# Attention scores on four groups of 32 rows, with a fourth query/key block and a new order of the attention pass

## The chip, the cores and the metric

The kernel runs on one core of one Trainium2 chip. The metric is the device time of one execution in microseconds.

## What is computed

32 images of 96x96 pixels become 36 patch tokens and a class token each (layer norm, linear, layer norm, positions); with 128 text tokens that is a sequence of 165 rows of 192 values. On it come an attention without softmax (the "linear" one), then the block that this change is about, then an MLP and a top-2 mixture of four experts:

```
h = concat(tokens(x), txt)                       # 32 x 165 x 192
h = h + linear_attention(layernorm(h))           # q k^T / sqrt(192) times v, no softmax
u = layernorm(h)
z = layernorm(u) * g + b
q, k, v = split(z @ in_w.T + in_b)               # 12 heads of 16
attn = softmax(q k^T / sqrt(16))                 # per image and head, 165 x 165
x1 = u + concat_heads(attn @ v) @ out_w.T + out_b
x2 = x1 + mlp(x1);  out = h + x2 + experts(layernorm(x2))
```

## The kernel before

**Stages.** Phase one makes the tokens and both attentions, phase two (from about 690 us) the MLP, routing and experts; the change touches phase one only. Phase one works on pairs of images: 165 rows of each, laid out as three tiles of 128 rows (one of text rows for each image, one with the 37 image-token rows of both at rows 0 and 64). There are 16 pairs. The code of each engine is written out by hand: a set-up with the patches, then `body(0)`, a hardware loop over pairs 1 to 14 and `last_body(15)`; on ScalarE pair 14 stands outside the loop. The engines meet in semaphores that count. There is no planner; the order of the lines in the four `body` functions is the order of work.

**What a pass does.** Body(i) does the softmax attention of pair i and, between its steps, the linear attention and layer norms of pair i+1 (`tokens_T`, `lin_y`, `lin_v`, `lin_m`, `lin_tokens`, `z_T`) and the statistics of pair i+2 (`tokens`). Scores of pair i are made in six units u: three tiles (`TILE_OF`) times two. Each has six heads. TensorE's `scores` (L1937) fills two banks of PSUM with 3 x 165 columns each; VectorE's `maxima` (L1394, one reduction of 990 elements) takes the row minima of the negated scores (`nb`); ScalarE's `exps` (L934) writes the exponentials to `PX` in six instructions; `transpose_probs` (L1970) transposes them on TensorE, 18 groups g of three 128x128 tiles, and the copies `PT` of the groups are shared by ScalarE (odd g) and VectorE (even g). Units with even u use banks 0 and 1, with odd u banks 2 and 3, so that one unit can be filled while the other is read. `contexts_T` (values times probabilities), `contexts` (back to rows), `normed_T` and `project` end a pair; `x1_out` adds the residual.

**Heads and rows.** The product of one head has a contraction of 16. Before, a matmul of `scores` takes a half of 64 rows with four heads, of which three are masked: `queries` (L1017) writes six versions of Q, each with one head of each half left (`own`), with six ScalarE instructions from two blocks of the product `queries_keys`; `keys` (L1404) writes K in five VectorE instructions from two blocks, one of them shared with queries. There are three blocks m of 128 columns: queries 0 to 7, keys 0 to 7, and the last four heads of both. Two 64-row halves of the array work at once.

```
rows = slice(64 * half, 64 * half + 64)
bank, col = 2 * (u % 2) + half, c * S
q, k = Q[rows, 2 * c + u % 2, :], K[rows, c // 2, :, (1 - half) * NIMG:(1 - half) * NIMG + S]
```

**GpSimd** makes the powers for the layer norms (`rstd`: 3 is that before the linear attention, 4 the two behind it, in one instruction) and the addition of the output bias to U (`residual`, UB, L760), on which `x1_out` depends. `w1_high` and `w1_low` split the MLP's and experts' first weights in two parts; two of them stand at the end of pair 14, the others in the last body. `keep_running` issues transposes that nobody reads.

## Time and profile before

| | |
|---|---|
| median of 3 runs (lowest, highest) | 1270.21 us (1269.87, 1274.73) |
| the profiled execution | 1270.14 us |
| its span in the profile | 1268.4 us |
| mean granted clock of TensorE | 0.987 |
| instructions | 27728 |
| busy: TensorE / VectorE / ScalarE / GpSimd | 1176.9 / 875.1 / 745.5 / 410.0 us |
| set-up and first pass / passes 1 to 14 / last pass / phase two | to about 103 / 39.6 us each / 33 us / from 690 us |

The span is that of the profile, and the time is 1.7 us longer, for what lies around it. Busy TensorE time is the union of its matmuls, which are pipelined and whose ends are modelled; it says when TensorE had work, not that it was at its peak. fp32 matmuls are issued as two instructions each. In the rows, L1879 is the helper through which all matmuls go and L1882 that of all transposes, so the names behind the line tell the operation: K,Q are scores, PX the transposes of probabilities, XAT,AT is `lin_y`, PT,VX is `contexts_T`, ZH,wqkr a block of queries and keys, ow,CNT is `project`.

### The profile page before, as it was taken

What the parts mean: (1) busy time and instruction counts of PE and PEld (TensorE: products, weight loads), DVE (VectorE), ACT (ScalarE), POOL (GpSimd) and SP (SyncE); (2) the same over time, 40 slices, a digit from 0 to 9 for tenths busy, and PEclk for the clock granted to TensorE, in tenths of its full rate; (3) what the DMA queues carried; (4) which work ended last, traced back from release to release, by engine and by line L of the source; (5) the groups of instructions that cost most, each with busy time, mean ns of one, the idle gap of its engine ahead of it and who ended that gap; (6) DMA issues with size and microseconds to landing.
All of it is one profiled execution on the core that took longest, in us unless ns stands there. A gap on an engine that the chain in (4) does not pass through costs nothing.

```text
span 1268.4 us, 27728 instructions
## 1 busy us (share of the span) xinstructions
PE 1176.9 (93%) x9709; PEld 1005.2 (79%) x9709; DVE 875.1 (69%) x2380; ACT 745.5 (59%) x1717; POOL 410.0 (32%) x402
## 2 busy tenths in 40 slices
PE   8899989999899998999998999999997999999995
PEld 7777777777777777777776899999886899988995
DVE  4756776667766677666776678777775776777774
ACT  4566555665556654566566755546563666666753
POOL 4520110101101011010100058777668444454454
PEclk8999999999999999999999999999998999999998
DMA  5148221012210122111400533437556566666672
GB/s 212 58 114 220 61 60 52 27 41 60 60 52 28 40 60 60 52 29 39 106 17 36 196 66 73 88 69 198 161 155 152 144 169 179 181 161 166 156 192 27
DMA packets 98554, 127.23 MB, mean 100 GB/s; under 512 B 9735, under 2 KB 90504, under 8 KB 94768
## 3 DMA queue, kind: packets, MB, share of 16 engines
q1 hardware_dynamic: 74911, 105.24, 27.4%
q0 software_dynamic: 23568, 21.06, 11.1%
q8 instruction: 39, 0.64, 0.2%
q14 instruction: 36, 0.29, 0.1%
HBM read 72.49 MB, written 53.72 MB: 100 GB/s over the span
## 4 chain that ended last, share of the span: by engine, by line
PE 39%; issue 35%; DVE 13%; POOL 7%; ACT 3%; DMA 1%; another core or an unknown queue 1%; DVEq 0%; POOLq 0%; ACTq 0%; SPq 0%
PE PS L1879 35%; PE PS L1882 4%; DVE K L1409 2%; POOL UB L765 2%; POOL rs L757 2%; DVE U L1311 1%; POOL expert_rows L861 1%; ACT GF L1184 1%; DVE st L1300 1%; DVE CNT L1438 1%; DVE ZS L1375 1%; DVE ZL L1374 1%; DVE X L1444 1%; DVE Z L1381 1%
## 5 line engine op out<-in xcount | busy, mean ns | idle before, releaser
L1879 PE MATMUL PS<-w2r,GH 128*120 (+1 forms) x828 | 247.8, 363 | 1.9 <-DVE GL L1604 0.7
L1879 PE MATMUL PS<-w2r,GL 128*120 (+1 forms) x828 | 208.4, 252 | 0.0
L898 POOL DMA_INDIRECT out<-YO,ids x94 | 155.8, 1657 | 160.9 <-DVE flag L1820 141.2
L757 POOL TENSOR_TENSOR rs<-ve,minus_half 128x3 f32<-128x3 f32 (+1 forms) x32 | 34.9, 1092 | 503.5 <-DVE ve L1365 343.9
L941 ACT ACTIVATE PX<-PS,nb 128x165 f32<-128x165 f32 x576 | 177.3, 419 | 28.5 <-DVE nb L1397 26.8
L1184 ACT ACTIVATE GF<-PS,b1c 128x480 f32<-128x480 f32 (+1 forms) x216 | 137.4, 637 | 93.6 <-PE PS L1879 77.3
L1879 PE MATMUL PS<-XH,w1r 128*128 128x480 f32 (+1 forms) x432 | 171.7, 400 | 14.5 <-ACT GF L1184 10.9
L1402 DVE COPY PT<-PS 128x384 f32<-128x384 f32 x144 | 79.8, 554 | 112.7 <-PE PS L1882 111.7
L1879 PEld LDWEIGHTS PS<-w2r,GH 128*120 128x120 f32 x828 | 150.5, 182 | 4.7 <-DVE GL L1604 3.2
L1879 PEld LDWEIGHTS PS<-w2r,GL 128*120 128x120 f32 x828 | 152.8, 185 | 0.0
L1882 PE MATMUL PS<-ident,PX 128*128 128x128 f32 x864 | 133.7, 282 | 14.9 <-ACT PT L916 12.3
L1397 DVE TENSOR_REDUCE nb<-PS 128x6 f32<-128x990 f32 x96 | 113.6, 1183 | 46.1 <-PE PS L1879 41.9
L1882 PEld LDWEIGHTS PS<-ident,PX 128*128 128x128 f32 x864 | 94.8, 141 | 52.3 <-issue 21.6
L1879 PE MATMUL PS<-XS,w1r 128*128 128x480 f32 (+1 forms) x432 | 127.6, 377 | 0.0
L1879 PEld LDWEIGHTS PS<-XH,w1r 128*128 128x128 f32 x432 | 82.9, 192 | 43.6 <-ACT GF L1184 28.3
L1614 DVE TENSOR_TENSOR GL<-GF,GH 128x480 fp32r<-128x480 f32 (+1 forms) x150 | 93.6, 629 | 32.1 <-ACT GH L916 28.4
L916 ACT ACTIVATE PT<-PS 128x384 f32<-128x384 f32 x144 | 73.8, 513 | 60.1 <-PE PS L1882 60.1
L1879 PE MATMUL PS<-K,Q 64*128 64x165 f32 (+1 forms) x1536 | 105.4, 313 | 1.5
L861 POOL DMA_INDIRECT expert_rows<-R,dest x88 | 95.0, 1080 | 33.2 <-issue 27.5
L1879 PEld LDWEIGHTS PS<-K,Q 64*128 64x128 f32 (+1 forms) x1536 | 80.1, 159 | 22.2 <-issue 12.6
L1026 ACT ACTIVATE Q<-PS,qb,own 128x330 f32<-128x330 f32 x96 | 53.1, 627 | 75.1 <-PE PS L1879 64.8
L1879 PEld LDWEIGHTS PS<-XS,w1r 128*128 128x128 f32 x432 | 81.3, 192 | 11.9
(295 smaller groups left out, 2279.1 us busy)
## 6 DMA issues: line engine op xcount, KB each, us to landing
w1r<-expert_w_parts SPq DMA_DIRECT2D x25, 1536.0 KB
expert_rows<-empty SPq DMA_DIRECT2D x45, 369.4 KB, 5.5
RT<-expert_rows SPq DMA_DIRECT2D x22, 369.4 KB
X<-x_scratch SPq DMA_DIRECT2D x11, 360.0 KB
out<-X POOLq DMA_DIRECT2D x11, 360.0 KB, 5.6
H<-in_txt SPq DMA_DIRECT2D x16, 192.0 KB
out<-H SPq DMA_DIRECT2D x16, 192.0 KB
x_scratch<-X SPq DMA_DIRECT2D x16, 192.0 KB
```

What stands on the lines that cost most here:

```text
L757: nc.gpsimd.tensor_tensor(rs[:, cols, :].rearrange("p a b -> p (a b)"), ve[:, cols, :].rearrange("p a b -> p (a b)"), eps_half[:, 0:n], AL ...
L861: nc.gpsimd.indirect_dma_start(listd[:, :], bass.IndirectOffsetOnAxis(ap=dest[:, n % 2, t, k:k + 1], axis=0), R[n % RBUF][:, t, :], None, ...
L898: nc.gpsimd.indirect_dma_start(out[:, :], bass.IndirectOffsetOnAxis(ap=ids[:, i, t:t + 1], axis=0), YO[:, i % 2, t, :], None, bounds_check ...
L916: return nc.scalar.activation(dst, src, ACT.Copy, scale=scale)
L941: last = nc.scalar.activation(PX[:, u % 2, c, to:to + S], PS[:, 2 * (u % 2) + r, c * S:(c + 1) * S], ACT.Exp, bias=nb[:, u, 3 * r + c:3 * ...
L1026: last = nc.scalar.activation(to, PS[:, qk_bank(m), 0:2 * SE].rearrange("p (b q) -> p b q", b=2)[:, :, 0:S], ACT.Identity, bias=qb[:, v:v ...
L1184: nc.scalar.activation(GF[:, m % 3, 0:n], PS[:, 2 + m % 2, 0:n], ACT.Gelu, bias=bias, scale=1.0).then_inc(gelu_ready, 1)
L1397: nc.vector.tensor_reduce(nb[:, u, :].rearrange("p (a s) -> p a s", a=2), src, AX_X, ALU.min).then_inc(max_ready, 1)
L1402: cp(*probT_views(g)).then_inc(probT_dve_ready, 1)
L1614: tt(GL[at][:, m, 0:n], GF[:, m % 3, 0:n], GH[at][:, m, 0:n].bitcast(F32), ALU.subtract).then_inc(hid_ready, 1)
L1879: return nc.tensor.matmul(o, l, r, start=start, stop=stop)
L1882: return nc.tensor.transpose(o, x, ident[0:rows, 0:rows])
```

## The change

1. Scores take four groups of 32 rows at once, each with two heads of which one is masked. A step s now makes a whole tile, twelve heads in all four banks, and there are three steps; `score_ps` counts twice in a step, and `maxima` and `exps` still work on half a step. A step s > 0 waits for both exponential blocks of the one before.
2. There are four blocks of queries and keys (bank 3 for the new one), made in the order 0, 1, 3, 2. Q has three versions, written by three ScalarE instructions, and K needs four VectorE instructions. Weights of the blocks grow from 3 to 4 x 128 columns, in the set-up too, where one zeroing of K goes. `project` writes banks 4 and 5 instead of 3 and 4, patch tile 7 bank 1.
3. GpSimd: the power of two norms (`rstd` 4) is split in two instructions, the one that Z needs (5) first; UB waits for XA of the next pair.
4. New order in the bodies of TensorE, ScalarE and VectorE. Among others `lin_in` and `x1_out` stand ahead of the maxima on VectorE, `tokens(i + 2)` ahead of `normedT` and the keys. The weight splits of pair 14 move into the last body, and so do more transposes by `keep_running` (35 to 52 in the last body).

TensorE, start of a pass in the loop, before: scores of one unit, values, scores of the second unit, then transposes of probabilities and of XA, and the third unit.

```order
L1879 MATMUL PS<-K,Q 128x165 [waits k_ready]
L1879 MATMUL PS<-K,Q 128x165 x5
L1879 MATMUL PS<-wvr,ZH 128x192 [waits q_ready]
...
L1879 MATMUL PS<-K,Q 128x165 [waits x1_ready,q_ready]
L1879 MATMUL PS<-K,Q 128x165 x5
...
L1882 MATMUL PS<-ident,PX 128x128 [waits prob_ready]
L1882 MATMUL PS<-ident,PX 128x128 x5
...
L1882 MATMUL PS<-ident,XA 128x128 [waits v_ready]
...
L1879 MATMUL PS<-K,Q 64x165 x12
```

Now (one row here is a matmul, which the trace shows as two instructions; the rest of the values is left out):

```order
L1865 MATMUL PS<-K,Q 128x165 [waits q_ready]
L1865 MATMUL PS<-K,Q 128x165 x3
L1865 MATMUL PS<-K,Q 128x165 [waits q_ready,k_ready]
L1865 MATMUL PS<-K,Q 128x165 x3
...
L1865 MATMUL PS<-K,Q 128x165 [waits q_ready]
L1865 MATMUL PS<-K,Q 128x165 x3
L1865 MATMUL PS<-wvr,ZH 128x192 [waits k_ready,q_ready]
...
L1868 MATMUL PS<-ident,PX 128x128 [waits prob_ready]
L1868 MATMUL PS<-ident,PX 128x128 x5
...
L1868 MATMUL PS<-ident,XA 128x128 [waits v_ready]
...
L1865 MATMUL PS<-K,Q 64x165 [waits prob_ready]
L1865 MATMUL PS<-K,Q 64x165 x23
```

The second unit is gone from between the values and the transposes; the next step of scores stands behind the third transpose and waits for the exponentials (`prob_ready`).

VectorE, end of a pass and start of the next, before: copies of the context (CNT), keys (K), statistics of the text (BN_STATS to ve), then the first reduction, X and XA.

```order
L1438 COPY CNT<-PS 128x384
L1409 TENSOR_SCALAR K<-PS,consts 32x2x37 [waits qk_ps]
L1409 TENSOR_SCALAR K<-PS,consts 32x2x165 x2
L1409 TENSOR_SCALAR K<-PS,consts 64x2x37 [waits qk_ps]
L1409 TENSOR_SCALAR K<-PS,consts 128x2x165
L1300 BN_STATS st<-H 128x6 [waits txt_in]
...
L1305 TENSOR_SCALAR ve<-mv 128x3 [waits dve_step]
...
L1397 TENSOR_REDUCE nb<-PS 128x6 [waits score_ps]
...
L1444 TENSOR_TENSOR X<-PS,UB 128x384 [waits x1_stored]
...
L1311 TENSOR_SCALAR XA<-H,mv,rs 128x192 [waits rstd_ready3]
```

Now, from the last context's product (CN) on:

```order
L1419 TENSOR_TENSOR CN<-PS,rec 128x192 [waits dve_step]
L1295 BN_STATS st<-H 128x6 [waits txt_in]
...
L1300 TENSOR_SCALAR ve<-mv 128x3 [waits dve_step]
L1424 COPY CNT<-PS 128x384 [waits cnT_ps]
...
L1404 TENSOR_SCALAR K<-PS,consts 128x2x37 [waits qk_ps]
L1404 TENSOR_SCALAR K<-PS,consts 128x2x165
L1404 TENSOR_SCALAR K<-PS,consts 128x2x37 [waits qk_ps]
L1404 TENSOR_SCALAR K<-PS,consts 128x2x165
...
L1306 TENSOR_SCALAR XA<-H,mv,rs 128x192 [waits rstd_ready3]
...
L1431 TENSOR_TENSOR X<-PS,UB 128x384 [waits x1_stored]
...
L1392 TENSOR_REDUCE nb<-PS 128x6 [waits score_ps]
```

The statistics moved ahead of CNT and the keys, one key instruction is gone, and XA and X stand ahead of the reductions.

The diff, cut to its core:

```diff
-QK_COLS = list(range(0, 128)) + list(range(D, D + 128)) + [w * D + 128 + 32 * half + e for half in range(2) for w in range(2)
-                                                           for e in range(32)]
+LAST_HEADS = (8, 9, 9, 8, 10, 11, 11, 10)
+QK_COLS = [w * D + e for heads in (range(8), LAST_HEADS) for w in range(2) for h in heads for e in range(h * HD, (h + 1) * HD)]
+QK_ORDER = (0, 1, 3, 2)
...
         def rstd(j, k):
             pool.wait_ge(var_ready[k], j + 1)
-            cols = slice(k - 1, k if k == 3 else k + 1)
...
+            nc.gpsimd.tensor_tensor(rs[:, k - 1, :], ve[:, k - 1, :], eps_half[:, 0:3], ALU.pow).then_inc(rstd_ready[k], 1)
...
+            if lin:
+                pool.wait_ge(xa_ready, i + 2)
             residual(i, first)
             if lin:
+                rstd(i + 1, 5)
                 rstd(i + 1, 4)
...
         def queries(j):
...
+            for v, m in enumerate((0, 0, 2)):
+                act.wait_ge(qk_ps, j * 4 + QK_ORDER.index(m) + 1)
...
         def body(i):   # ScalarE
             exps(i, 0)
+            exps(i, 1)
             probsT(i, 1)
             xaT(i + 1)
-            exps(i, 1)
+            probsT(i, 3)
             lin_y(i + 1, 0)
             lin_y(i + 1, 1)
-            probsT(i, 3)
             exps(i, 2)
             probsT(i, 5)
+            lin_v(i + 1)
+            probsT(i, 7)
             exps(i, 3)
-            probsT(i, 7)
-            lin_v(i + 1)
             lin_m(i + 1)
+            probsT(i, 9)
             exps(i, 4)
-            probsT(i, 9)
             probsT(i, 11)
...
         def scores(i, s):   # TensorE
+            t = TILE_OF[s]
+            if s > 0:
+                pe.wait_ge(prob_ready, i * 6 + 2 * s)
             for c in range(3):
+                if s == 0:
+                    pe.wait_ge(k_ready, i * 2 + 2)
+                    pe.wait_ge(q_ready, i * 3 + max(c + 1, 2))
+                for g in range(4):
+                    rows = slice(32 * g, 32 * g + 32)
+                    q, k = Q[rows, c, :], K[rows, c // 2, :, (1 - g % 2) * NIMG:(1 - g % 2) * NIMG + S]
                     if t < 2:
+                        last = mm(PS[:, g, c * S:c * S + S], q[:, D * t:D * t + P], k[:, t, :])
                     else:
                         for b in range(2):
+                            last = mm(PS[64 * b:64 * b + 64, g, c * S:c * S + S], q[:, D * b + P:D * b + D], k[:, b, :])
+                    if c == 2 and g % 2 == 1:
+                        last.then_inc(score_ps, 1)
...
         def last_body(i):   # ScalarE
             exps(i, 0)
             exps(i, 1)
+            w1_high(1)
             probsT(i, 1)
...
             exps(i, 3)
+            w1_high(2)
             probsT(i, 7)
-            exps(i, 4)
             probsT(i, 9)
             probsT(i, 11)
+            exps(i, 4)
             exps(i, 5)
```

## Rows read from the trace of the kernel before

**Rows 1.** Page, busy time by engine.

```profile
PE 1176.9 (93%) x9709; PEld 1005.2 (79%) x9709; DVE 875.1 (69%) x2380; ACT 745.5 (59%) x1717; POOL 410.0 (32%) x402
```

**Rows 2.** Windows: us, busy (x instructions) by engine, granted clock, DMA.

```profile
301.20:340.78 39.58, 36.38 (x376) 29.08 (x376) 26.89 (x67) 23.06 (x67) 3.91 (x5) 1.00 0.18 48
```

**Rows 3.** Waits in one pass: us, times, longest.

```profile
DVE PT L1402 <- PE PS L1882: 7.0, 4, 2.7
ACT Q L1026 <- PE PS L1879: 4.4, 1, 4.4
...
ACT MT L916 <- PE PS L1879: 1.9, 1, 1.9
```

**Rows 4.** Timeline, start of a pass: start, us, engine, line [idle before <-releaser].

```profile
299.67 1.48 DVE L1409 TENSOR_SCALAR K<-PS,consts 32x330 f32<-32x330 f32 x3
...
301.20 1.11 PE L1879 MATMUL PS<-K,Q 64*128 64x165 f32 x12
...
302.56 0.47 PE L1879 MATMUL PS<-wvr,ZH 128*128 128x192 f32 x2 [0.25 <-ACT Q L1026]
...
302.83 1.19 DVE L1397 TENSOR_REDUCE nb<-PS 128x6 f32<-128x990 f32 x1 [0.35 <-issue]
...
303.93 0.55 DVE L1444 TENSOR_TENSOR X<-PS,UB 128x384 f32<-128x384 f32 x1
...
304.05 1.84 ACT L941 ACTIVATE PX<-PS,nb 128x165 f32<-128x165 f32 x6 [1.54 <-DVE nb L1397]
...
304.66 1.51 DVE L1311 TENSOR_SCALAR XA<-H,mv,rs 128x192 f32<-128x192 f32 x3
...
304.89 1.73 POOL L765 TENSOR_TENSOR UB<-U,consts 128x192 f32<-128x192 f32 x3 [1.48 <-DVE X L1445]
...
305.94 0.88 PE L1882 MATMUL PS<-ident,PX 128*128 128x128 f32 x6
```

**Rows 5.** Timeline, first pass, VectorE.

```profile
66.34 0.96 DVE L1311 TENSOR_SCALAR XA<-H,mv,rs 128x192 f32<-128x192 f32 x3 [0.54 <-POOL rs L757]
```

**Rows 6.** Timeline, middle of the pass.

```profile
308.12 1.07 PE L1879 MATMUL PS<-K,Q 64*64 64x165 f32 x24
...
309.51 2.39 PE L1879 MATMUL PS<-XAT,AT 128*128 128x330 f32 x8
...
316.86 0.73 ACT L916 ACTIVATE VL<-PS 128x384 f32<-128x384 f32 x2
...
326.78 0.55 DVE L1352 TENSOR_TENSOR H<-PS,H 128x384 f32<-128x384 f32 x1
...
329.53 0.56 DVE L1402 COPY PT<-PS 128x384 f32<-128x384 f32 x1
...
329.62 1.89 PE L1879 MATMUL PS<-PT,VX 128*32 128x165 f32 x48
...
330.94 0.96 DVE L1381 TENSOR_SCALAR Z<-H,mv,rs 128x192 f32<-128x192 f32 x3 [0.85 <-POOL rs L757]
```

**Rows 7.** Timeline, end of the pass.

```profile
336.43 0.36 DVE L1432 TENSOR_TENSOR CN<-PS,rec 128x192 f32<-128x192 f32 x1
...
337.03 0.56 PE L1879 MATMUL PS<-ZH,wqkr 128*128 128x332 f32 x2
...
337.89 0.48 PE L1879 MATMUL PS<-ZH,wqkr 128*128 128x332 f32 x2
...
338.37 2.36 DVE L1409 TENSOR_SCALAR K<-PS,consts 32x74 f32<-32x74 f32 x5
...
338.66 2.11 PE L1879 MATMUL PS<-ow,CNT 128*128 128x192 f32 x12
```

**Rows 8.** Chain of waits, last pass: start, us, what.

```profile
658.48 2.26 PE PS L1879 x20
...
681.73 0.77 PE PS L1879 x16
...
690.25 0.57 ACT XH L916
```

More of the change, by code:

```diff
@@ L195, in build_program @@
     qb = sb(one, "qb", [P, 6])
-    Q = sb(one, "Q", [P, 6, 2 * D])
+    Q = sb(one, "Q", [P, 3, 2 * D])
+    sb(one, "spare_one", [P, 3 * 2 * D - 4 * P])
     K = sb(one, "K", [P, 2, 2, NIMG + S])
@@ L801, in _ @@
         patch_tokens(4)
+        rstd(0, 5)
         rstd(0, 4)
@@ L1072, in body @@
             probsT(i, 15)
+            probsT(i, 17)
             contextsT(i, 0)
-            probsT(i, 17)
             contextsT(i, 1)
             zT(i + 1)
-            if not more:
-                w1_high(1)
-                w1_high(2)
             queries(i + 1)
@@ L1142, in _ @@
         body(0)
-        with act.Fori(1, PAIRS - 2) as i:
+        with act.Fori(1, PAIRS - 1) as i:
             body(i)
-        body(PAIRS - 2, more=False)
         last_body(PAIRS - 1)
@@ L1278, in pair_biases @@
             dve.wait_ge(const_in, 16)
-            steps.link(tt(qkb[:, :], qkb[:, :], PS[:, 1, 2 * D:2 * D + 3], ALU.add))
+            steps.link(tt(qkb[:, :], qkb[:, :], PS[:, 1, 2 * D:2 * D + 4], ALU.add))
             tt(vb[:, :], vb[:, :], PS[:, 1, D:2 * D], ALU.add).then_inc(setup_dve, 1)
-            ts(qb[:, 0:4], own[:, :], qkb[:, 0:1], None, ALU.mult)
-            ts(qb[:, 4:6], own[:, 0:2], qkb[:, 2:3], None, ALU.mult)
+            ts(qb[:, 0:2], own[:, 0:2], qkb[:, 0:1], None, ALU.mult)
+            ts(qb[:, 2:3], own[:, 0:1], qkb[:, 2:3], None, ALU.mult)
             nc.vector.memset(mx[:, 0, 0:1], 0.0).then_inc(h1_stored, 1)
@@ L1404, in keys @@
         def keys(j, m):
-            dve.wait_ge(qk_ps, j * 3 + (0, 3, 1)[m])
-            def part(src, to, at, key, n):
-                cols = PS[src, qk_bank(m), 0:2 * SE].rearrange("p (b q) -> p b q", b=2)[:, :, key:key + n]
-                return ts(K[to, m - 1, :, at:at + n], cols, qkb[src, m:m + 1], -HEAD_SCALE, ALU.add, ALU.mult)
-            if m == 1:
-                part(slice(64, P), slice(64, P), 0, P, NIMG)
-                last = part(slice(0, P), slice(0, P), NIMG, 0, S)
-            else:
-                part(slice(96, P), slice(64, 96), 0, P, NIMG)
-                part(slice(32, 64), slice(0, 32), NIMG, 0, S)
-                last = part(slice(96, P), slice(64, 96), NIMG, 0, S)
+            dve.wait_ge(qk_ps, j * 4 + QK_ORDER.index(m) + 1)
+            for at, key, n in ((0, P, NIMG), (NIMG, 0, S)):
+                cols = PS[:, qk_bank(m), 0:2 * SE].rearrange("p (b q) -> p b q", b=2)[:, :, key:key + n]
+                last = ts(K[:, m // 2, :, at:at + n], cols, qkb[:, m:m + 1], -HEAD_SCALE, ALU.add, ALU.mult)
             last.then_inc(k_ready, 1)
@@ L1485, in body @@
             contexts(i, 2)
-            normedT(i)
-            keys(i + 1, 2)
-            keys(i + 1, 1)
-            if not more:
-                w1_low(1)
             if more:
                 tokens(i + 2)
+            normedT(i)
+            keys(i + 1, 1)
+            keys(i + 1, 3)
         def last_body(i):
             maxima(i, 0)
+            maxima(i, 1)
             x1_out(i - 1)
             values(i)
-            maxima(i, 1)
             probsT(i, 0)
+            probsT(i, 2)
             maxima(i, 2)
-            probsT(i, 2)
             maxima(i, 3)
             probsT(i, 4)
+            w1_low(1)
+            probsT(i, 6)
+            probsT(i, 8)
+            maxima(i, 4)
+            maxima(i, 5)
             w1_low(2)
-            probsT(i, 6)
-            maxima(i, 4)
-            probsT(i, 8)
             probsT(i, 10)
-            maxima(i, 5)
             probsT(i, 12)
@@ L1553, in _ @@
         dve.wait_ge(qk_zeroed, 1)
-        keys(0, 2)
         keys(0, 1)
+        keys(0, 3)
         tokens(1)
@@ L1907, in biases @@
             pe.wait_ge(lin_bias_ready, 1)
-            for m in range(3):
+            for m in range(4):
                 for k in range(2):
@@ L2128, in body @@
         def body(i, first=False):
+            if first:
+                pe.wait_ge(yvar_ready, PTILES - 1)
             scores(i, 0)
             values(i)
-            if first:
-                pe.wait_ge(yvar_ready, PTILES - 1)
-            scores(i, 1, first)
+            if not first:
+                pe.wait_ge(x1_ready, i)
             transpose_probs(i, 0)
```

138 lines of the change are left out of this document (52 added, 86 removed).

## The prediction

> **What bounds the kernel now.** I read the page first for the balance, then the stretches, then the waits and the timeline of one pass. TensorE is busy 1176.9 of the 1268.4 us [rows 1], so a reader might stop there. The stretches are more telling: one pass of the attention loop (one pair of images) takes 39.58 us, in which TensorE is busy 36.38, VectorE 26.89, ScalarE 23.06 [rows 2]. No engine is full, and "busy" counts pipelined ends. The waits of that pass show TensorE and its partners waiting in turns: VectorE's copies of probabilities wait 7.0 us for TensorE, ScalarE's queries 4.4 [rows 3]. It is a ring of hand-overs, and a pass lasts as long as its longest ring. I cut the ring at the moment when VectorE's last key instruction ends (301.14) and call it 0; the next one is at 340.73 [rows 4, 7]. All T below count from there. Three marks of the pass before: the first transposes of probabilities at T 4.8 (305.94), the second transposed context product ends at T 30.4 (329.62 + 1.89) and the ring closes at T 39.6, so the parts are 4.8, 25.6 and 9.2 us [rows 4, 6, 7].
>
> **Part 1: the score products.** A unit before has 12 instructions (6 matmuls in two passes) on 64-row halves and takes 1.11 us [rows 4]; with the last one's 0.30 us latency off, that is 0.81/11 = 74 ns each. The middle units, on 64x64 quarters, issue 24 in 1.07 us [rows 6]: 0.77/23 = 33 ns each. So two pieces of the array side by side give 74 ns, four give 33 ns. After the change a step is 24 instructions on four 32-row groups, or 48 on eight pieces (four row groups, two column halves) for the middle tile. I price each of the three steps at 1.1 us, the row of four pieces. Bounds: 24 at 74 ns is 2.0 us; below, eight pieces at 17 ns and four at 33 give again 1.1. TensorE then has three units where it had six, 3 x 1.05 = 3.2 us less work a pass, against one more query/key block, five matmuls from 337.03 to 337.89 or 0.86 us [rows 7].
>
> What this rests on: the trace's loads of 128 columns come 74 ns apart on two row groups, so loads of different row groups run beside each other. The Trainium skill, "TensorE: Matmul & The Clock Gate", section on LDWEIGHTS, says that a load costs its columns over 1.2, whatever its rows: an estimate of 107 ns for 128 columns, and if loads were one at a time a step would be 24 x 107 ns = 2.6 us and the change a loss. The trace does not agree with loads one at a time.
>
> **Part 2: queries and keys.** Queries: six activations become three, and ScalarE waits 4.4 us there anyway [rows 3]: nothing on the path. Keys: five instructions in 2.36 us become four; the one left out has 330 elements, 0.57, leaving 1.8. It is on the path: -0.57.
>
> **Part 3: order on VectorE.** The statistics of the next text stood behind the keys: from 301.14 to the reduction at 302.83 are 1.69 us, of which 0.35 are marked issue (the loop's branch) and 1.34 the statistics [rows 4]. Now they stand in the tail, ahead of the context's last copies: +1.34 there, and gone from behind the keys. Then come the normalisation (XA), the residual (X), and only then two reductions. XA's three instructions take 1.51 us in the loop, but 0.96 in the first pass, where they run before GpSimd's UB additions [rows 4, 5]; in the loop UB's 1.73 us run beside them. The change lets UB wait for XA, so I take 0.96. Left beside it, it would cost 0.55 more a pass.
>
> **Part 4: the walk of the new pass.** VectorE: branch 0.35, XA 0.96, X 0.85 (0.73 to the next start, and its drain), reduction 1.19 makes T 3.4. ScalarE's exponentials of the first half (1.84) end at 5.25, and the transposes start at 5.3: **+0.5** against 4.8. TensorE stands idle from about 3.7 (project until 0.5, scores 1.1, values 2.26 [rows 8]), so the first step's price is covered by VectorE up to some 1.6 us.
> From 5.25: second exponentials 1.84 (7.1); the second score step must wait for them, as it overwrites both halves: 0.2 + 1.1 (8.4); transposes 0.3; the 330-column product 2.4 with 0.15 to its second half's copy, copy 0.45 (11.65); exponentials 1.84 (13.5); copy 0.5, value copies 0.73, copy 0.5, exponentials 1.84 (17.1); third score step 0.2 + 1.1, reduction 1.19, exponentials 1.84 (21.5); transposes 0.55, copy 0.56 (22.6); the H addition with its statistics, 326.78 to 329.53, 2.75 (25.4); copy 0.56, two transposes 0.9 (26.9), context product 1.89 = 28.8 [rows 6]. The part lasts 23.5 us where it was 25.6: **-2.1**. It gains because three score units and their switches of array shape left TensorE's queue, and because the two waits of ScalarE between exponentials shrink (1.9 us for MT alone [rows 3]).
> Tail: from there Z is ready and not waited for (0.85 for GpSimd's power before [rows 6]), so the last CN is done 4.4 later, where it took 5.3 (to 336.43 + 0.36 [rows 7]); statistics 1.34, two CNT copies 1.05, keys 1.8: T 37.45, with 0.1 for starts. **-0.5** against 9.2. TensorE's projection (2.11 us [rows 7], 0.2 to start) then ends at T 0.5, and the scores start behind it, as the walk has it. The split of GpSimd's power of six columns (1.33) into two of three costs nothing: z_out stands behind a copy of probabilities.
> A pass: 37.5, so -2.1.
>
> **Part 5: ends.** First pass: the fourth block delays the scores by 0.8, but the two exponential blocks end as early as they must; its gain is 1.6. The 13 common passes: 13 x 2.1 = 27.3. The last loop pass has no statistics, so their move gives nothing: 1.8. Last body: ScalarE's high parts of two weight blocks and VectorE's subtractions move in between the exponentials, where ScalarE has to be on time. There T 0 before is 657.1 (the values' start 658.48 [rows 8] less the 1.4 that lie between 301.14 and 302.56 in the loop [rows 4]). By the same kind of walk the second context product ends at T 28.2, where it was at 682.5 - 657.1 = 25.4 [rows 8]: +2.7. Everything behind 690.25 [rows 8] is unchanged. Moved copies of high weights gained nothing before: they stood where ScalarE waited.
> Sum: -1.6-27.3-1.8+2.7 = **-28.0 us**. The profiled execution took 1270.14 against a median of 1270.21, so the sum holds for the median: 1242.
>
> **Rivals.**
> *Scores pace themselves* (loads or passes of row groups overlap only in pairs). For: no row has four row groups; 64-row halves give 74 ns. Against: four quarters give 33. Price: 24 x 74 ns + 0.3 = 2.1 us and 48 x 33 ns + 0.3 = 1.9; the first step is half covered, the two others add 1.0 and 0.8: a pass of 39.2, that is 15 x 1.7 = 25.5 given back, **1268**.
> *The gate on both halves* (slower side). Before, one half of the score banks is filled while the other is read. Now every step waits for two exponential blocks, 3.7 us, and TensorE has to live on transposes and the linear attention of the next pair, whose copies sit on ScalarE between those same exponentials. The middle is a chain of some 20 hand-overs; I gave each 0 to 0.1 us. If each costs 0.1 more the 2.1 us are gone, and at 0.15 more a pass is 0.9 longer than before: 15 x 0.9 + 2.7 = 16, **1286**. For: copies of probabilities wait 7.0 us a pass [rows 3]. Against: VectorE and ScalarE are each idle for over 12 us [rows 2].
> The Trainium skill, "TensorEngine Tiling (Array Packing)", section "PSUM Bottleneck", warns that tiling speeds TensorE and not the emptying of PSUM; the rows of the reductions and exponentials agree, since they cost the same as before.
> *A shorter ring* (the moved work fills waits better, and the last body doesn't lose): 36.6 a pass and nothing lost at the end: 15 x 3.0 = 45, **1225**.
>
> **How the numbers follow.** Forecast 0.62 (1242; its own range 1230 to 1258 is +-1 us a pass), shorter ring 0.14, pace of scores 0.10, gate 0.08, something between forecast and no change 0.06. A measurement of this kernel tells about 0.5% (6.4 us) from no change. Faster: 0.62 + 0.14 + 0.05 = 0.81. Same: most of the score rival and what is left between, 0.10. Slower: 0.09. The range for 8 in 10, 1226 to 1262, leaves out half of the shorter ring, the gate and most of the score rival.
>
> **What the new profile should show.** Passes 37.5 us apart; the score steps 24 and 48 instructions in about 1.1 us (over 1.7: rival one); XA in 0.96, UB behind it; TensorE idle some 1.6 us ahead of the first transposes, with the granted clock at 1.00 as in the pass before [rows 2]; a last body longer by 2 to 3 us. I am wrong if a pass is above 38.6, or if the steps are cheap and ScalarE and VectorE wait longer than before in the middle (rival two).

## The result, and the profile after

The changed kernel takes **1227.51 us** (median of 4 runs, 1225.09 to 1228.78); the kernel before, run beside it on the same chip, 1270.97 us (4 runs). The ratio is 0.9651, 95% interval 0.9625 to 0.9677, and the medians differ by 43.5 us, where 28 were forecast. Ratios here and below are of the means of the fast runs; one run of the kernel before, in the second group of the experiments, was a slow one (1421.43 us at a granted clock of 0.75) and is not among them. The span of the profiled execution is 1226.3 us, against 1268.4. Its busy time, as in [rows 1]:

```profile
PE 1142.6 (93%) x9810; PEld 982.8 (80%) x9810; DVE 854.3 (70%) x2364; ACT 718.1 (59%) x1669; POOL 413.5 (34%) x417
```

Where the time came from, stretch by stretch, cut in both traces at the end of VectorE's last key instruction:

| stretch | before | after | forecast |
|---|---|---|---|
| set-up, to T 0 of the first pass | 62.13 | 63.45 | +0.8, in the next row |
| first pass | 41.4 | 38.2 | -1.6 |
| each of the 13 common passes, mean | 39.56 | 36.27 | -2.1 |
| last loop pass | 39.2 | 36.2 | -1.8 |
| last body, to XH | 33.2 | 38.4 | +2.7 |
| behind it | 578.2 | 578.5 | 0 |

The sum is 1.3 - 3.2 - 13 x 3.29 - 3.1 + 5.2 + 0.3 = -42.3 us; the spans differ by 42.1. So each pass gains half as much again as forecast, and the last body loses twice as much. Of the set-up's 1.3 us a part is clock: from 59 to 63 us the granted clock is 0.57 in the changed kernel, with 0.50, the lower of its two levels, in the middle of it; the kernel before has 1.00 from 58 to 62.

The windows of one pass (against [rows 2]), of the last body, and of five microseconds in it:

```profile
355.54:391.81 36.27, 33.92 (x383) 27.44 (x382) 25.46 (x66) 21.31 (x63) 4.24 (x6) 1.00 0.19 52
609.39:647.85 38.46, 31.07 (x363) 25.61 (x362) 24.45 (x45) 21.36 (x58) 1.69 (x3) 0.96 0.02 8
614.40:619.40 5.00, 3.67 (x17) 3.13 (x17) 2.14 (x6) 3.92 (x10) 1.69 (x3) 0.66 0.15 51
```

TensorE is busy 33.92 us where it was 36.38, so 2.5 us of its work are gone from a pass that is 3.3 shorter. The granted clock is 1.00 in the pass, and 0.66 shortly after the last body's start; within those five microseconds it is 0.50 for 3.2 us (615.72 to 618.95). The waits of the same pass (us, times, longest), against [rows 3]:

```profile
DVE PT L1397 <- PE PS L1868: 7.0, 7, 2.4
...
ACT Q L1025 <- PE PS L1865: 4.1, 2, 2.5
ACT PX L944 <- DVE nb L1392: 3.9, 2, 3.6
```

The start of the pass on the timeline (T 0 is 355.54), against [rows 4]:

```profile
354.12 1.42 DVE L1404 TENSOR_SCALAR K<-PS,consts 128x74 f32<-128x74 f32 x4
...
354.46 2.12 PE L1865 MATMUL PS<-ow,CNT 128*128 128x192 f32 x12
...
355.46 0.95 DVE L1306 TENSOR_SCALAR XA<-H,mv,rs 128x192 f32<-128x192 f32 x3
...
356.51 1.12 PE L1865 MATMUL PS<-K,Q 32*128 32x165 f32 x24
...
356.73 0.56 DVE L1431 TENSOR_TENSOR X<-PS,UB 128x384 f32<-128x384 f32 x1 [0.33 <-PE PS L1865]
...
357.21 0.35 DVE L1432 TENSOR_TENSOR X<-PS,UB 128x192 f32<-128x192 f32 x1
...
357.67 2.28 DVE L1392 TENSOR_REDUCE nb<-PS 128x6 f32<-128x990 f32 x2
...
357.70 1.71 POOL L765 TENSOR_TENSOR UB<-U,consts 128x192 f32<-128x192 f32 x3 [3.49 <-DVE X L1432]
...
360.79 0.88 PE L1868 MATMUL PS<-ident,PX 128*128 128x128 f32 x6 [0.98 <-ACT PX L944]
```

The 24 score instructions take 1.12 us. They end at 357.63, and VectorE, whose X ends at 357.56, begins its reduction at 357.67: two engines arrive there within 0.1 us of each other. Both had to wait for the projection, which ends at 356.58. XA takes 0.95, and no gap is marked between the keys and it, though the loop's branch lies there. The other two score steps, the two context products, and the tail with the statistics, against [rows 6, 7]:

```profile
362.57 1.11 PE L1865 MATMUL PS<-K,Q 32*64 32x165 f32 x48
...
372.49 1.12 PE L1865 MATMUL PS<-K,Q 32*128 32x165 f32 x24
...
381.34 0.87 PE L1868 MATMUL PS<-ident,PX 128*128 128x128 f32 x6 [0.58 <-DVE PT L1397]
...
382.14 1.89 PE L1865 MATMUL PS<-PT,VX 128*32 128x165 f32 x48
...
387.88 0.36 DVE L1419 TENSOR_TENSOR CN<-PS,rec 128x192 f32<-128x192 f32 x1
...
388.15 0.87 DVE L1295 BATCH_NORM_STATS2 st<-H 128x6 f32<-128x192 f32 x3
...
389.49 0.55 DVE L1424 COPY CNT<-PS 128x384 f32<-128x384 f32 x1
```

Which of the two engines sets the pace from the tail to the first reduction is told by the chain of waits. In the kernel before it goes through VectorE's keys:

```profile
339.25 0.57 DVE K L1409
```

In the changed kernel it stays on TensorE for 6.8 us without a gap, through the query and key blocks, the projection and the scores, and touches neither the statistics nor the keys:

```profile
387.10 1.83 PE PS L1865 x10
388.93 0.44 PE PS L1868 x4
389.37 4.55 PE PS L1865 x46
...
393.94 1.20 DVE nb L1392
```

The marks of the pass are therefore T 5.25 (first transposes, 360.79), T 28.5 (382.14 + 1.89) and T 36.27; the parts are 5.25, 23.24 and 7.8 us, where 5.3, 23.5 and 8.7 were forecast. The last body, against [rows 8]:

```profile
615.72 1.12 PE L1868 MATMUL PS<-ident 128*128 128x128 f32 x4 [2.01 <-DVE VX L1386]
...
616.63 2.40 PE L1868 MATMUL PS<-ident,PX 128*128 128x128 f32 x9
...
629.94 1.81 DVE L1437 TENSOR_TENSOR w1r<-rw,w1r 128x768 fp32r<-128x768 f32 x2
...
632.37 0.84 PE L1868 MATMUL PS<-ident,PX 128*128 128x128 f32 x6 [1.50 <-DVE PT L1397]
```

Ahead of the first transposes TensorE waits 2.01 us for the values' copy; then nine instructions of transposes take 2.40 us, where six take 0.88 in the pass. Later it waits 1.50 for a copy that stood behind a weight subtraction.

### The profile page after: what moved, and what is told of

The parts are those of the page before. It is cut to its first block, busy times and chain, and to the rows that moved or that the text cites. A ratio compares the mean times of both kernels' runs of the same rounds, so it can differ in the third digit from the quotient of the medians.

```text
span 1226.3 us, 27879 instructions
## 1 busy us (share of the span) xinstructions
PE 1142.6 (93%) x9810; PEld 982.8 (80%) x9810; DVE 854.3 (70%) x2364; ACT 718.1 (59%) x1669; POOL 413.5 (34%) x417
## 4 chain that ended last, share of the span: by engine, by line
PE 66%; DVE 12%; issue 9%; POOL 6%; ACT 5%; another core or an unknown queue 1%; DMA 1%; POOLq 0%; ACTq 0%; SPq 0%; DVEq 0%
PE PS L1865 52%; PE PS L1868 13%; POOL expert_rows L864 4%; ACT PX L944 2%; DVE nb L1392 2%; ACT GF L1179 1%; DVE PT L1397 1%; POOL out L852 1%; DVE st L1354 1%; DVE H L1350 1%; POOL lex L857 1%; DVE ZS L1370 1%; DVE ZL L1369 1%; DVE H L1347 1%
## 5 line engine op out<-in xcount | busy, mean ns | idle before, releaser
L944 ACT ACTIVATE PX<-PS,nb 128x165 f32<-128x165 f32 x576 | 174.1, 417 | 59.3 <-DVE nb L1392 59.3
L758 POOL TENSOR_TENSOR rs<-ve,minus_half 128x3 f32<-128x3 f32 x48 | 40.5, 854 | 423.2 <-DVE ve L1359 318.2
L1868 PE MATMUL PS<-ident,PX 128*128 128x128 f32 x864 | 136.8, 284 | 30.9 <-ACT PX L944 17.0
L1392 DVE TENSOR_REDUCE nb<-PS 128x6 f32<-128x990 f32 x96 | 112.1, 1184 | 39.8 <-PE PS L1865 38.4
L1233 ACT ACTIVATE YO<-PS,cs 120x192 f32<-120x192 f32 x94 | 39.3, 419 | 80.3 <-PE PS L1865 69.1
L919 ACT ACTIVATE GH<-GF 128x480 fp32r<-128x480 f32 (+1 forms) x141 | 83.5, 592 | 4.5
L1865 PE MATMUL PS<-XL,w1r 128*128 128x480 f32 (+1 forms) x216 | 81.1, 376 | 0.0
```

Source lines behind the costliest of these rows:

```text
L758: nc.gpsimd.tensor_tensor(rs[:, k - 1, :], ve[:, k - 1, :], eps_half[:, 0:3], ALU.pow).then_inc(rstd_ready[k], 1)
L919: return nc.scalar.activation(dst, src, ACT.Copy, scale=scale)
L944: last = nc.scalar.activation(PX[:, u % 2, c, to:to + S], PS[:, 2 * (u % 2) + r, c * S:(c + 1) * S], ACT.Exp, bias=nb[:, u, 3 * r + c:3 * ...
L1233: nc.scalar.activation(YO[:, at, t, :], PS[0:TB, 4 + t, 0:D], ACT.Copy, scale=cs[:, i, t:t + 1]).then_inc(high_out, 1)
L1392: nc.vector.tensor_reduce(nb[:, u, :].rearrange("p (a s) -> p a s", a=2), src, AX_X, ALU.min).then_inc(max_ready, 1)
L1865: return nc.tensor.matmul(o, l, r, start=start, stop=stop)
```

## The experiments

They ran in three groups, each beside the kernel before: in the first group it takes 1258.06 us, in the second 1267.69, in the third 1258.66. The first group had one chip, the second and the third another one, the same for both. What compares is the ratio to the kernel before in the same group. "The changed kernel on the same chip" means its ratio (0.9651, again 0.9639) times that time. Pass lengths are from one GpSimd addition UB to the next; "XH at" is where the attention phase ends in the profiled execution (690.25 in the kernel before, 647.8 in the changed one), so that it can be compared without what lies behind. It still holds the set-up, which differs a little from run to run: the first UB of the profiled executions lies at 67.1 to 70.2 us.

| kernel | median us (runs) | ratio [95%] | a pass | XH at |
|---|---|---|---|---|
| changed, again | 1223.0 (4) | 0.9639 [0.9615, 0.9663] | 36.27 | 647.3 |
| dose0 | 1228.07 (4) | 0.9759 [0.9743, 0.9775] | 37.10 | 660.4 |
| dose12 | 1242.07 (4) | 0.9872 [0.9849, 0.9895] | 37.94 | 673.4 |
| tokens_back | 1251.03 (4) | 0.9945 [0.9929, 0.9962] | 37.97 to 40.75 | 681.0 |
| tokens_back_busy | 1247.53 (4) | 0.9845 [0.9822, 0.9869] | 37.99 | 668.2 |
| w1_back | 1216.05 (4) | 0.9665 [0.9649, 0.9681] | 36.27 | 647.7 |
| last_new | 1217.23 (4) | 0.9604 [0.9584, 0.9623] | 36.27 | 641.0 |
| act14 | 1218.46 (4) | 0.9605 [0.958, 0.9629] | 35.96 | 645.7 |
| best | 1205.13 (5) | 0.9572 [0.9554, 0.959] | 35.97 | 637.5 |
| x_first_wait | 1224.94 (4) | 0.9735 [0.9716, 0.9754] | 36.93 | 656.8 |
| x_first_free | 1231.8 (4) | 0.9792 [0.9771, 0.9813] | 37.48, one 38.93 | 664.4 |
| before_tokens | 1262.28 (7) | 1.0034 [1.0023, 1.0045] | 39.82 | 694.4 |

### dose0 and dose12: what a score step costs

The matmuls of the first step (dose0), or of the second and third (dose12), are issued twice, the second time over the same result.

```diff
-            for c in range(3):
+            for rep, c in [(rep, c) for rep in range(2 if s == 0 else 1) for c in range(3)]:
...
-                    pe.wait_ge(q_ready, i * 3 + max(c + 1, 2))
+                    pe.wait_ge(q_ready, i * 3 + (3 if s == 0 else max(c + 1, 2)))
...
-                    if c == 2 and g % 2 == 1:
+                    if rep == (1 if s == 0 else 0) and c == 2 and g % 2 == 1:
                         last.then_inc(score_ps, 1)
```

dose12 has `s > 0` in these places. In dose0 the first step also waits for the third version of Q from its first matmul on. That costs nothing in the trace: the step starts 0.92 us behind the keys' end, in the changed kernel 0.97. In dose12 the changed wait has no effect.

> The changed kernel, with every matmul of the first score step issued twice (same result), in all 16 passes. One step is six rounds of 0.14 us, so TensorE gets 0.84 us more a pass. Theory A (the forecast's: VectorE's XA, X and reduction cover the first step up to some 1.6 us): 0 to +2 us in all. Theory B (read from the new trace, where project ends, the step starts at once and the reduction starts on its end: the tail of the ring runs through TensorE): 16 x 0.84 = +13 us.

> The changed kernel, with every matmul of the second and third score step issued twice, which brings TensorE's score work a pass to 5 steps where it has 3 now. Theory A (score steps of the middle lie on the ring, as the walk has them): 2 x 0.84 x 16 = +27 us. Rival (ScalarE's and VectorE's chain of copies and exponentials paces the middle, TensorE has room): under +10 us.

dose0's first step and the reduction behind it:

```profile
360.61 1.96 PE L1865 MATMUL PS<-K,Q 32*128 32x165 f32 x48
...
362.61 2.29 DVE L1392 TENSOR_REDUCE nb<-PS 128x6 f32<-128x990 f32 x2 [0.95 <-PE PS L1865]
```

The second helping adds 0.84 us to the step, VectorE now waits 0.95 for it, and the pass is 37.10 instead of 36.27, longer by just that 0.84. In all it costs 13.9 us against the changed kernel's 1214.2 on this chip, for 13 expected of theory B. The forecast's cover of 1.6 us is not there: the step is on the ring in full. The two steps of dose12 become 1.95 and 1.96 us and the pass 1.67 longer, so they are on the ring in full too (27.9 us in all, for 27 expected). Together the three steps move the pass by what they cost. Read backwards, and as an estimate: had four pieces side by side been no faster than two (steps of 2.1, 2.1 and 1.9 us, the forecast's first rival), a pass would be some 2.8 us longer, and little of the 3.3 us gained would be left. By that estimate the gain hangs on the four row groups running beside each other. No run has the new order with 64-row halves, or the row groups in the old order.

### tokens_back and tokens_back_busy: the statistics in the tail

On VectorE the statistics of pair i+2 go back behind the keys, all else as in the changed kernel. The second kernel adds 14 transposes that nobody reads (into bank 5), ahead of the first transposes of a pass.

```diff
-            if more:
-                tokens(i + 2)
             normedT(i)
             keys(i + 1, 1)
             keys(i + 1, 3)
+            if more:
+                tokens(i + 2)
...
                 pe.wait_ge(x1_ready, i)
+                keep_running(5, 14)     # tokens_back_busy alone
             transpose_probs(i, 0)
```

> The changed kernel, with the text's statistics (tokens) on VectorE moved back behind the keys. Theory: the tail is 1.3 us shorter, but XA, which now stands first in the next pass, has to wait for the statistics (1.3) and GpSimd's power (0.85), so X and both reductions come some 2 us later: +0.8 us a pass, +11 in all. Rival (the place of the statistics doesn't matter, since TensorE's project ends the tail anyway): within 3 us of the changed kernel.

> The kernel tokens_back (1251 us where the changed one is some 1214 on the same chip) with 14 idle transposes (1.5 us) ahead of the first transposes of a pass, where TensorE stood idle 2.8 us. In tokens_back 38.0 us was a pass at granted clock 1.00, and about a third of the passes took 39.3 to 40.8 at 0.92 to 0.96. Theory A (the long idle time costs clock): all passes 38.0 at 1.00, 10 to 15 us faster than tokens_back. Rival (the long passes come from transfers or from elsewhere): no change, or slower by what the transposes cost.

tokens_back, end of a pass, start of the next, and two passes in windows:

```profile
407.90 0.56 DVE L1424 COPY CNT<-PS 128x384 f32<-128x384 f32 x1 [1.16 <-PE PS L1868]
...
412.57 0.96 DVE L1306 TENSOR_SCALAR XA<-H,mv,rs 128x192 f32<-128x192 f32 x3 [0.97 <-POOL rs L758]
...
417.28 1.54 PE L1868 MATMUL PS<-ident,PX 128*128 128x128 f32 x6 [2.71 <-ACT PX L944]
```

```profile
180.66:220.18 39.52, 35.44 (x383) 28.56 (x381) 25.48 (x66) 21.39 (x63) 4.21 (x7) 0.96 0.17 48
373.65:414.40 40.75, 36.69 (x384) 29.79 (x381) 25.48 (x66) 21.51 (x63) 4.22 (x7) 0.92 0.17 46
```

Taken out of the tail, the statistics shorten it by almost nothing: VectorE then waits 1.16 us for the transposed context. From the last CN to the end of the keys are 3.51 us, against 3.57. Behind the keys they cost themselves and 0.97 us of GpSimd's power in addition: the first reduction starts 3.9 us behind the keys instead of 2.1. That is the 1.7 us of the 37.99 us passes, twice what was expected of the order. Then TensorE is idle for 2.7 us ahead of the first transposes in every pass, and five of the 13 passes have a granted clock of 0.92 to 0.96 and last 39.3 to 40.75 us. In these five the clock is at 0.50 for some 3 to 7 us, beginning within about 1 us of the end of that wait; the other eight have 1.00 throughout. tokens_back_busy fills that idle time and does nothing else:

```profile
255.13:293.12 37.99, 35.47 (x398) 28.95 (x396) 25.49 (x66) 21.31 (x63) 4.22 (x6) 1.00 0.18 50
```

All its passes take 37.97 to 38.01 us. The ratio falls from 0.9945 to 0.9845, which is 12.7 us, and XH comes 12.8 us earlier. The two kernels ran on different chips, but the traces agree with the ratios: 8.6 us of it lie in those five passes, 1.5 ahead of the first UB, the rest at the end. So about a third of tokens_back's 37 us was the clock, and the rest mostly the order. The changed kernel's idle stretch at that place is 0.98 us, and its passes keep 1.00.

### before_tokens: the same move in the kernel before

```diff
+            if more:
+                tokens(i + 2)
             normedT(i)
...
             keys(i + 1, 1)
...
-            if more:
-                tokens(i + 2)
```

> The kernel before the change with the statistics of the text moved ahead of normedT and the keys, as in the change, and nothing else. Theory (that order suits the new structure only: in the old one the reduction waits for the scores anyway, so it starts some 0.4 us sooner, while the tail grows by 0.8): +0.4 us a pass, 5 us slower than before. Rival (the move is a gain of its own, the statistics leave the ring): 0.5 to 1 us a pass faster.

```profile
339.84 0.55 DVE L1437 COPY CNT<-PS 128x384 f32<-128x384 f32 x1
...
344.46 1.19 DVE L1397 TENSOR_REDUCE nb<-PS 128x6 f32<-128x990 f32 x1 [1.21 <-PE PS L1879]
```

The ratio is 1.0034 [1.0023, 1.0045], 3 to 6 us more, as expected, and a pass is 39.82 against 39.58. From CN's end to the keys' end are 4.65 us instead of 3.94: CNT no longer waits, but that wait was only 0.53 and the statistics are 1.34. Behind the keys no more than 0.48 is won, since the reduction needs the scores, which need the last key and take 1.11: it starts 1.21 behind the keys instead of 1.69. So the move that is worth 1.7 us a pass in the new structure costs 0.24 in the old one, where the statistics filled a wait for the scores.

### x_first_wait and x_first_free: XA, X and GpSimd's UB

Both put the residual X ahead of XA on VectorE; the second also takes away GpSimd's new wait for XA.

```diff
-            lin_in(i + 1)
             x1_out(i - 1)
+            lin_in(i + 1)
...
-            if lin:                          # x_first_free alone
-                pool.wait_ge(xa_ready, i + 2)
```

> The changed kernel with X ahead of XA on VectorE, GpSimd's UB still waiting for XA. Theory: X can start only when project ends (1.2 us after the keys), so the 0.95 us of XA, done in that gap now, come behind it: reductions 0.8 us later, 37.1 us a pass (if TensorE's longer idle time costs no clock), +12 us in all. Rival (the place of XA is free): 36.3.

> As x_first_wait, but GpSimd's UB no longer waits for XA, so it runs beside XA. Theory (they share a way to the SBUF, as the 0.96 and 1.51 us of XA before the change say): XA 1.5 us, 0.55 us more a pass than x_first_wait, 37.6 us, +8 us. Rival (GpSimd costs XA nothing): the same as x_first_wait.

X, XA and UB of one pass in x_first_wait, then in x_first_free:

```profile
359.45 0.56 DVE L1431 TENSOR_TENSOR X<-PS,UB 128x384 f32<-128x384 f32 x1 [1.17 <-PE PS L1865]
...
360.19 0.95 DVE L1306 TENSOR_SCALAR XA<-H,mv,rs 128x192 f32<-128x192 f32 x3
...
361.36 1.70 POOL L765 TENSOR_TENSOR UB<-U,consts 128x192 f32<-128x192 f32 x3 [4.41 <-DVE XA L1306]
```

```profile
365.37 1.51 DVE L1304 TENSOR_SCALAR XA<-H,mv,rs 128x192 f32<-128x192 f32 x3
...
365.59 1.74 POOL L765 TENSOR_TENSOR UB<-U,consts 128x192 f32<-128x192 f32 x3 [3.47 <-DVE X L1430]
```

X first costs 0.66 us a pass, and 9 us in all by XH, 11 to 12 by the ratios (12 expected): X waits 1.17 us for the projection, and XA, which has nothing to wait for, no longer fills that time. With UB free to run beside XA, its three instructions take 1.51 us instead of 0.95, and the pass is longer by just that, 37.48 against 36.93. So the effect that the forecast read from [rows 4, 5] is real and worth 0.55 us a pass. But in the changed kernel the order alone should secure it: UB waits for X (3.49 us above), X stands behind XA, and the added wait has nothing left to do in the loop. That follows from the code and the trace; the changed kernel without that wait alone was not tried.

### w1_back, last_new: the last body

w1_back puts ScalarE's high parts of weight blocks 1 and 2 and VectorE's subtraction of block 1 back to the end of pair 14; the subtraction of block 2 stays in the last body. last_new does this too and reorders the last body: X ahead of the maxima, no wait for the values' copy ahead of the first transposes, exponentials 2 and 4 a copy earlier on ScalarE, the subtraction of block 2 ahead of the copy and the two reductions that it stood behind, and the idle transposes shared out anew (34 for 32 in these places).

```diff
             queries(i + 1)            # ScalarE, pair 14
+            if not more:
+                w1_high(1)
+                w1_high(2)
...
             keys(i + 1, 3)            # VectorE, pair 14
+            if not more:
+                w1_low(1)
...
+            x1_out(i - 1)             # VectorE, last_new
             maxima(i, 0)
             maxima(i, 1)
-            x1_out(i - 1)
...
             values(i)                 # TensorE, last_new
-            pe.wait_ge(v_ready, i + 1)
-            keep_running(6, 4)
             pe.wait_ge(x1_ready, i)
             transpose_probs(i, 0)
             transpose_probs(i, 1)
+            pe.wait_ge(v_ready, i + 1)
+            keep_running(6, 2)
```

> The changed kernel, with the high parts of weight blocks 1 and 2 (ScalarE) and the low part of block 1 (VectorE) put back at the end of pass 14, as before the change; block 2's low part stays in the last body. The last body took 33.2 us before and 38.5 after. Theory A (ScalarE's 1.6 us copies stand between exponentials and delay them): 3 to 5 us faster than the changed kernel, about 1223. Rival (the order of TensorE's steps and its extra idle transposes cost it): within 1 us of the changed kernel.

> The changed kernel with a last body of another order: weight blocks 1 and 2 high and 1 low at the end of pass 14; X of pair 14 ahead of the reductions; the first transposes no longer wait for the values' copy; each score step as soon as the exponentials allow; block 2 low after the sixth copy. In the changed kernel the last body takes 38.5 us, with a stretch in which the granted clock is 0.66 after TensorE waited 2.0 us for the values' copy. Theory (waits of my list and the lost clock make it long, not the added idle transposes): the second context product ends at T 24 instead of 30.7 and the granted clock stays 1.00: 5 to 7 us faster than the changed kernel. Rival (the chain of exponentials sets it): under 2 us.

w1_back, block 2's subtraction and the wait for the copy behind it, then two windows; then two windows of last_new:

```profile
628.62 1.81 DVE L1439 TENSOR_TENSOR w1r<-rw,w1r 128x768 fp32r<-128x768 f32 x2
...
631.05 2.13 PE L1871 MATMUL PS<-ident,PX 128*128 128x128 f32 x9 [1.97 <-DVE PT L1399]
```

```profile
613.00:618.00 5.00, 3.65 (x17) 3.20 (x17) 2.14 (x6) 2.47 (x8) 1.68 (x3) 0.66 0.15 51
628.00:633.00 5.00, 3.02 (x19) 2.20 (x17) 3.46 (x5) 4.44 (x14) 0.00 (x0) 0.84 0.00 0
```

```profile
608.00:641.50 33.50, 29.78 (x366) 24.37 (x365) 23.75 (x44) 18.80 (x55) 2.07 (x6) 1.00 0.03 9
610.00:615.00 5.00, 3.63 (x47) 3.05 (x54) 3.95 (x7) 3.95 (x13) 1.71 (x3) 1.00 0.15 51
```

w1_back is not faster (0.9665 for the changed kernel's 0.9651, 1.8 us, inside the intervals; XH at 647.7 for 647.8, but from the UB of pair 14's pass to XH it takes 73.8 us for 72.6). The 1.2 us more are clock: behind its second wait nine transposes take 2.13 us and a context product 2.68, where 1.68 and 1.89 are usual, so by this estimate the body would be as long as in the changed kernel. Sending back the high parts and block 1's subtraction gives nothing. The first wait is still 2.01 us, with the clock at 0.66 behind it, and later there is a wait of 1.97 us with 0.84 around it. That second wait is for a copy right behind block 2's subtraction, as the 1.50 in the changed kernel is, and w1_back left this subtraction where it was. So it does not clear VectorE's subtractions as a whole.

In last_new TensorE waits at most 1.3 us there, and the clock is 1.00 throughout. From the UB of pair 14's pass (573.32; 575.23 in the changed kernel) to XH are 67.7 us instead of 72.6: -4.9, and -4.4 by the ratio to the changed kernel in the same group. That is just short of the 5 to 7 expected, and the second context product ends at T 25.8, where T 24 was expected. The last body's loss is thus in the order of its hand-overs, block 2's subtraction among them, with the clock as a part of the price: nine transposes at 2.40 instead of 1.68 us and four at 1.12 instead of 0.60 are 1.2 us. How much each of last_new's moves gives was not taken apart.

### act14: the ring's last hand-over of the middle

Copy 14 of the probabilities goes from VectorE to ScalarE, since the transposes at 381.34 wait 0.58 us for VectorE.

```diff
-ON_ACT = (1, 3, 5, 7, 9, 11, 13, 15, 17)
+ON_ACT = (1, 3, 5, 7, 9, 11, 13, 14, 15, 17)
```

> The changed kernel with copy 14 of the transposed probabilities on ScalarE instead of VectorE, where it stood behind the 2.7 us of lin_out while TensorE waited 0.6 to 0.8 us for it. Theory (that wait is on the ring): about 0.35 us a pass, 5 us in all. Rival (next in line is ScalarE's own copy 15, or the tail): 0 to 1 us.

```profile
379.27 0.93 PE L1868 MATMUL PS<-ident,PX 128*128 128x128 f32 x6 [0.25 <-ACT PT L919]
```

The wait falls to 0.25, a pass to 35.96 (-0.31), the ratio to 0.9605, 4 to 6 us less than the changed kernel (5 expected). The intervals of the two ratios overlap; it is the passes that show the gain. VectorE's copies wait 7.0 us a pass for TensorE, and yet at this one place it is TensorE that waited for a copy.

### best: both, and the first weight block earlier

best is last_new with act14, and the first weight block's split moved between the exponentials of the last body.

> The order of last_new with copy 14 on ScalarE (act14), and in the last body block 0's high part ahead of copy 9 and its low part ahead of copy 16, where VectorE stood idle 2.1 us. Theory: the gains add, since they lie in different passes: 0.31 us in each of 14 passes and 5.1 + 0.8 us at the end, ratio to before 0.954 to 0.956, where the changed kernel has 0.964 to 0.965. Rival (one takes the other's wait): 0.960.

```profile
247.21:283.18 35.97, 33.96 (x382) 27.43 (x383) 24.95 (x65) 21.73 (x64) 4.34 (x6) 1.00 0.19 53
```

1205.13 us against 1258.66: ratio 0.9572 [0.9554, 0.959], some 8 to 10 us better than the changed kernel. The ratio is above the expected 0.954 to 0.956 by 0.1 to 0.3%, between theory and rival, but nearer to the theory. XH comes at 637.5, 10 us earlier, which is the whole of what the two gains were to give. It is the fastest version of this study.

### after_again: the changed kernel on the second chip

> The changed kernel itself once more, on the chip of this group, so that the others can be compared with it. Ratio to before as measured, 0.965.

1223.0 against 1267.69 us, ratio 0.9639 [0.9615, 0.9663]: the ratio repeats within the interval, and the pass is 36.27 again.

## Why the prediction was right, and where it was off

**Direction and mechanism: right.** The ring of hand-overs was the bound, and it shrank. But 1227.5 us lies inside the range of 1226 to 1262 by 1.5 us only, outside the forecast's own 1230 to 1258, and nearer to the rival of a shorter ring (1225) than to 1242. That it is inside at all owes something to luck: the passes gained some 15 us more than forecast, and the last body gave 2.5 of that back. Three marks were forecast and two met: the first part is 5.25 us (forecast 5.3), the middle 23.24 (23.5).

**Score steps: right.** 1.12, 1.11 and 1.12 us for a forecast of 1.1. The first rival (scores pace themselves) fell by these rows. That rival's price was also too low: it called the first step half covered and then counted it as nothing, where dose0 shows it in full. By the rule of the Trainium skill ("TensorE: Matmul & The Clock Gate", section on LDWEIGHTS), taken one load at a time, a step is an estimated 2.6 us; the trace has less than half of that. The second rival (a gate on both halves) fell too: the waits between VectorE's copies and TensorE are 7.0 us, as before, VectorE's waits sum to 10.3 us a pass instead of 12.1 and ScalarE's to 15.0 instead of 16.6, and the 1.9 us that ScalarE waited for MT are gone. Emptying PSUM costs what it did: two reductions take 2.28 us and twelve exponentials 3.57.

**The cover of the first score step: wrong.** The step that failed is "so the first step's price is covered by VectorE up to some 1.6 us". dose0 shows no cover at all. I had measured the slack at TensorE's idle time ahead of the transposes, behind the values. But the ones who need the scores are VectorE's reductions, and by the walk itself these were ready at T 2.2, some 0.5 behind the scores' end. The projection also ends later against T 0 than "T 0.5": at 356.58, T 1.04, because VectorE, by whose keys T is counted, is done earlier. So TensorE is idle ahead of the first transposes for 0.98 us, not 1.6. At 1.1 us a step this error moved no term; with a dearer step it would have been the largest one.

**The start: right by two errors that cancel.** The 0.35 us of loop branch, which I carried over, is not on the ring: XA begins as the keys end. In its place X waits 0.33 for the projection. The first reduction starts at T 2.13, for a forecast of 2.2.

**The tail: mis-sized by 0.9 us a pass, the largest error, and laid on the wrong engine.** Forecast 8.7, measured 7.8. The step that failed is the walk from the last CN on: "statistics 1.34, two CNT copies 1.05, keys 1.8", then "branch 0.35, XA 0.96, X 0.85", one chain on VectorE. It makes 6.45 us from the last CN's end to the first reduction, where the kernel before has 5.63. Measured are 5.70, and 0.33 of them are X's wait for the projection. VectorE's own work is a full microsecond shorter than the walk had it: from CN's end to the keys' end are 3.6 us instead of 4.25, and the branch is not there. Four keys take 1.42 us and not 1.8: I had subtracted one instruction's 0.57 from 2.36 as if the rest stayed as it was, but one pair of keys (74 and 330 elements on 128 rows) takes 0.71. So VectorE falls behind TensorE as the one that ends last, and the blocks, the projection and the scores set the stretch, as the chain above shows. By the same chain the keys, which part 2 has "on the path", are no longer on it; with 0.33 us of waiting ahead of X, shorter keys should give nothing more, which no run tried.

tokens_back shows what I had not seen: without the statistics VectorE would wait 1.16 us in the tail, so they stand there nearly free and save 1.7 us at the start. The rest of the pass's error is smaller: the last CN is done 4.2 us behind the product instead of 4.4, and the middle is 0.3 shorter. All this makes -3.3 instead of -2.1 a pass, 13 x 1.2 = 16 us. The rival of a shorter ring had 36.6 a pass and was the nearer one there.

**XA at 0.95: right in size, wrong in cause.** x_first_free loses the 0.55 us again when UB runs beside it. The wait that I credited looks redundant in the loop; the order XA, X, UB should do it alone, which no run shows.

**Ends.** Set-up and first pass: -1.9 together for -1.6. Last loop pass: -3.1 for -1.8. Last body: +5.2 for +2.7, mis-sized, and for a reason that is right only in part: "ScalarE's high parts ... and VectorE's subtractions move in between the exponentials". The second context product ends at T 30.7 instead of 28.2. w1_back shows that sending back the high parts and block 1's subtraction recovers nothing. Block 2's subtraction does stand ahead of a copy for which TensorE waits 1.50 us, and the wait for the values' copy, 2.01 us with the low clock behind it, was in no term of the forecast. last_new shows that some 5 us lie in these hand-overs together. A walk that gives every transpose its full-speed duration cannot see the 1.2 us that the clock took.

**Order against row groups.** Each piece was tried by itself in the changed kernel: doubling the steps would cost 2.5 us a pass; the statistics' place is worth 1.7, XA ahead of X 0.66, UB apart from XA 0.55. These sum to more than 3.3, since each is measured with the others in place, and before_tokens shows that one of them is a loss in the old structure.

## What to carry to other kernels

Measure a resource's slack where its product is needed (here VectorE's reduction), not where the engine next stands idle, and issue its work twice to see it: if the pass grows by the whole of the addition, there is no cover. Moving work into a wait pays only if a wait of that size is there in the new structure; so judge the order and the edit that frees time together, and undo each with the other in place. In a dense kernel look at the granted clock behind TensorE's longest waits, and at whether an engine that you shortened still ends last.

## What the runs showed of the hardware

- **Pieces of the array.** Two row groups of 64: 12 instructions in 1.11 us. Four of 32: 24 in 1.12. Eight pieces of 32x64: 48 in 1.11. One step's worth issued twice takes 0.84 us more, so one instruction on four pieces costs 35 ns in a stream, on eight 17.
- **Single idle stretches and the clock.** A wait of 2.01 us of TensorE in the last body stands ahead of a stretch granted 0.66 (nine instructions of transposes 2.40 us, 1.68 in a pass), one of 1.97 us in w1_back ahead of 0.84 and less. In dose12's profiled execution the last body has the same 2.01 and a 1.97, and the clock stays at 1.00. Waits of 2.7 us came with 1.3 to 2.8 us more in five of 13 passes of tokens_back and with nothing in the others; x_first_free, with 2.2 us, has one such pass of 13 (38.93 at 0.96). Passes with 0.98 and 1.64 us have 1.00 everywhere. The same idle time does not always have the same price, and in tokens_back transposes that nobody reads removed it.
- **VectorE beside GpSimd.** Three fp32 instructions of 192 elements take 0.95 us alone and 1.51 beside GpSimd's additions.
- **From group to group.** What lies behind XH, the same instructions in all of these kernels, takes 578 us in the first comparison, 566 to 568 in the first and third group and 571 to 575 in the second, while the attention passes agree within 0.01 us. The kernel before varies by 1% too. The second and third group ran on the same chip, so the chip alone does not make the difference. That part moves more than 100 GB/s for most of its length, a pass 52; whether the memory is the reason was not tried.
